# First expert's result through ScalarE and GpSimd in a two-layer recurrent kernel, with every step placed anew

## The reference, cut to what matters

```
xn = layernorm(x)
s  = softmax(mask_diagonal(q/H @ k.T)) @ v            # q, k, v are projections of xn
p  = softmax(xn @ gate); keep the two largest, divide by their sum      # gates, 8 experts
y  = sum over e of gate_e * (relu(xn @ W1_e + b1_e) @ W2_e + b2_e)      # all 8 experts are computed
x  = x + s * silu(y)
xn = layernorm(x)
s  = mamba(rmsnorm(xn)) + xn        # conv, silu, 16 states: st = st * exp(delta*A) + delta*B*u, y = sum(st * C)
f  = expert chosen by nearest centroid (top 1), layernorm + 128x512x128 relu MLP
x  = x + s * silu(alpha * f + (1 - alpha) * xn)
```

## Time and profile before

| | us |
|---|---|
| median of 3 runs (963.87 to 964.8) | 964.21 |
| profiled execution, own time | 966.05 |
| its span, first to last instruction | 964.2 |
| DVE busy | 786.6 (82%) |
| PE busy, PEld busy | 831.5 (86%), 571.5 (59%) |
| ACT busy, POOL busy | 630.8 (65%), 601.5 (62%) |
| granted TensorE clock, mean | 0.941 |

### The profile page before, as it was taken

The page is one execution under the profiler, slowest core; times in us unless marked ns, Lnnn a source line. Parts: engine busy times, 40 slices in busy tenths (PEclk is TensorE's granted clock), DMA queues, the critical chain, the costliest instruction groups (busy, mean ns, idle before and its releaser), DMA issues. The chain is left out here.

```text
span 964.2 us, 15734 instructions
## 1 busy us (share of the span) xinstructions
PE 831.5 (86%) x4576; PEld 571.5 (59%) x4576; DVE 786.6 (82%) x1503; ACT 630.8 (65%) x1379; POOL 601.5 (62%) x556
## 2 busy tenths in 40 slices
PE   5987798998799978998799969997899865876995
PEld 3773376775477745775577646864577544544552
DVE  3234637989988998899998998899889999978994
ACT  2434645878668776878577866877687854675561
POOL 0010202758857695958766795759685888778664
PEclk9987799999999999999999999999999998876997
DMA  7200103224323243324322342334331433243441
GB/s 263 95 12 1 34 12 96 78 66 121 117 66 101 90 116 109 88 77 137 102 78 78 100 125 79 88 94 114 97 100 70 124 112 97 77 108 119 138 121 45
DMA packets 79430, 90.29 MB, mean 94 GB/s; under 512 B 8450, under 2 KB 49906, under 8 KB 78834
## 3 DMA queue, kind: packets, MB, share of 16 engines
q1 hardware_dynamic: 77298, 85.07, 28.9%
q0 software_dynamic: 2048, 4.20, 1.5%
HBM read 52.96 MB, written 13.04 MB: 68 GB/s over the span
## 5 line engine op out<-in xcount | busy, mean ns | idle before, releaser
L1502 POOL TENSOR_TENSOR st<-st,Cs 128x512 f32<-128x512 f32 x249 | 316.6, 1285 | 154.7 <-DVE st L1325 152.7
L961 ACT ACTIVATE dA<-delta,Aneg 128x512 f32<-128x512 f32 x256 | 176.9, 720 | 13.6 <-POOL du L1463 9.3
L1325 DVE TENSOR_TENSOR_SCAN st<-dA,b_row 128x512 f32<-128x512 f32 x123 | 148.8, 1210 | 9.3 <-POOL y L1509 7.3
L1325 DVE TENSOR_TENSOR_SCAN st<-dA,dbu 128x512 f32<-128x512 f32 x128 | 154.7, 1209 | 2.0 <-PE yacc L905 1.9
L1509 POOL TENSOR_TENSOR y<-y,st 128x512 f32<-128x512 f32 x105 | 138.8, 1322 | 3.9
L841 PEld LDWEIGHTS work<-w_w2a,hid 128*128 128x128 f32 x1024 | 121.3, 192 | 22.7 <-DVE delta L1293 7.0
L835 PE MATMUL work<-xnT,w_w1a 128*128 128x512 f32 x256 | 134.7, 630 | 0.0
L905 PE MATMUL yacc<-st,w_ident 128*128 128x512 f32 x208 | 116.0, 647 | 14.7 <-POOL st L1502 9.6
L841 PE MATMUL work<-w_w2a,hid 128*128 128x128 f32 x1024 | 125.7, 276 | 2.6 <-DVE delta L1293 2.0
L961 ACT ACTIVATE hsT<-work,hs 128x128 f32<-128x128 f32 x352 | 99.9, 367 | 41.6 <-PE work L866 41.3
L866 PEld LDWEIGHTS work<-xsT,hs 128*128 128x128 f32 x704 | 93.1, 199 | 54.8 <-issue 37.3
(11 more groups left out here) (191 smaller groups left out, 1319.0 us busy)
## 6 DMA issues: line engine op xcount, KB each, us to landing
Cs<-c_dram SPq DMA_DIRECT2D x128, 256.0 KB, 3.6
hs<-w_w1f SPq DMA_DIRECT2D x88, 258.0 KB, 2.3
xs_in<-xs_dram SPq DMA_DIRECT2D x16, 256.0 KB, 2.9
ys_dram<-ys SPq DMA_DIRECT2D x16, 256.0 KB, 3.3
w_w1f<-in_w1f_dram SPq DMA_DIRECT2D x1, 2064.0 KB, 8.3
x_in<-in_x_dram SPq DMA_DIRECT2D x8, 256.0 KB, 4.9
w_w2f<-in_w2f_dram SPq DMA_DIRECT2D x1, 2048.0 KB, 12.4
kept_dram<-x_tok SPq DMA_DIRECT2D x8, 256.0 KB, 3.6
```

The costliest lines, as they stand in the source:

```text
L961: return nc.scalar.activation(out, in_, func, **k)
L1325: V.tensor_tensor_scan(state(s), dA[:, s % DECAYS], (dbu0, rows_bank(n, b))[h][:], 0.0, ALU.mult, ALU.add).then_inc(sig["scan"], 1)
L1502: G.tensor_tensor(state(s), state(s), Cs[:, b.of(NS, n) % C_BUFS], ALU.mult).then_inc(sig["P"], 1)
```

## The change

Expert 0 leaves DVE. Where DVE did four fused multiply-adds out of PSUM, ACT now evicts the bank with `Copy` and the gate as its scale into `gated`, a view of the first tile of `prob` (its attention weights have been read by then), and POOL adds that to `acc`.

```diff
+        gated = prob[:, 0].rearrange("p (i d) -> p i d", i=NT)
 # ACT
+                elif name == "m" and i == 0:
+                    filled(act, g, step, b)
+                    filled(act, g, ("p", NT - 1), b)
+                    act.wait_ge(sig["gates"], b.of(1, 1))
+                    for t in range(NT):
+                        last = go(gated[:, t], w[:, t * 128:(t + 1) * 128], ACT.Copy, scale=gates[:, t, 0:1])
+                    last.then_inc(fr, 1)
                 elif name == "s":
                     act.wait_ge(sig["smax"], b.of(NT, i + 1))
+                    if i == 0:
+                        since(act, sig["acc"], b.of(E + 1, -E))
 # DVE, step gate
                         filled(dve, g, ("gT", 0), b + -1)
+                        emptied(dve, g, ("m", 0), b + -1)
 # DVE, step m
-                elif name == "m":
-                    if i == 0:
+                elif name == "m" and i > 0:
+                    if i == 1:
                         dve.wait_ge(sig["gates"], b.of(1, 1))
-                        emptied(dve, g, ("b2", 0), b)
-                    else:
-                        dve.wait_ge(sig["acc"], b.of(E + 1, i))
+                    dve.wait_ge(sig["acc"], b.of(E + 1, i))
                     filled(dve, g, step, b)
 # POOL
+                elif name == "m" and i == 0:
+                    emptied(pool, g, ("b2", 0), b)
+                    emptied(pool, g, step, b)
+                    G.tensor_tensor(acc[:], acc[:], gated, ALU.add).then_inc(sig["acc"], 1)
```

Every row of `ROWS` and every entry of `OWN` has a new place, shift or both, and some have another bank. Two of the rows:

```diff
-    ("A", "m", 0, 0.31929, 6, 1, 7, 0),
-    ("A", "m", 7, 0.96705, 7, 1, 6, 0),
+    ("A", "m", 0, 0.30730, 0, 4, 0, 0),
+    ("A", "m", 7, 0.93254, 7, 1, 2, 0),
...
```

More of the change, by code:

```diff
@@ L335 @@
     ("A", 0): (
[4 rows of a table removed]
[4 rows of a table added]
     ),
     ("H", 0): (
-        -1.18779, -1.13573, -1.09164, -1.08398, -1.03594, -0.89467, -0.96660, -0.83534, -0.78966, -0.81791, -0.81272, -0.56441,
-        -0.78084, -0.73569, -0.76396, -0.85924, -0.68237, -0.67607, -0.57595, -0.60328, -0.61173, -0.84375, -0.80983, -0.51997,
-        -0.45727, -0.71044, -0.78180, -0.65968,
+        -1.10650, -1.13980, -1.09852, -0.77033, -0.97924, -0.88306, -0.94385, -0.78471, -0.76988, -0.74369, -0.71077, -0.54599,
+        -0.71041, -0.70861, -0.68303, -0.96618, -0.66433, -0.64530, -0.60176, -0.71869, -0.62037, -0.84304, -0.70132, -0.51193,
+        -0.51164, -0.46084, -1.07428, -0.69329,
     ),
     ("A", 1): (
[4 rows of a table removed]
[4 rows of a table added]
     ),
```

## The result

The changed kernel takes 984.24 us (median of 4 runs, 978.14 to 987.09), the kernel before 964.06 us beside it: a ratio of 1.0199 (1.015 to 1.0249). The forecast of 963.4 us was 21 us too low, and the time lies outside the range of 955 to 969.5.

A forecast was written before the change was run, and what follows sets the result against it. It took a steady stage as a loop of PE's leg (C `y` to `m1`) and DVE's leg (`m1` to C `y`); -2.7 at the start and +1.9 over five periods gave -0.8, so 963.4 us, 8-in-10 range 955 to 969.5.

The forecast's parts named there:

- Elsewhere: Stretches before the first stage, the last two stages and SP's DMAs: each put at 0, with small allowances.
- The period: Steady stage from `m1` to `m1`: 0.37 us longer (-0.1 to 0.9), +1.9 us over five periods.
- leg 1: PE's part of a steady stage, from C `y` to `m1`: 39.4 us, to change by -1.08.
- leg 2: DVE's part of a steady stage, from `m1` to the next C `y`: 66.4 us, to change by +1.45.
- the 0.48 at `xi0`: DVE's wait ahead of `xi0` after `m1`, to be filled: -0.48 us against `scan13`'s +1.93.
- the -1.08: PE between `a0` and `m1` loses `Ah6` (0.86 us) and `b7` (0.22 us) from its list.
- The start of the first stage: PE's 3.26 us wait ahead of `Fh0` goes; `b2` comes 3.1 us sooner, leaving -2.7 us at stage end.
- the relief: Rival, steady stages: less DVE work shortens each of five periods by 1.24 us; 955.3 us, chance 0.29.
- ACT's evictions: Four evictions on ACT in a steady stage: 1.14 us of work, 1.6 us of slack, 0 taken.
- POOL's add: One add on POOL, behind `p9` and ahead of `e4`: 1.25 us of work, 0 taken, 1.25 a stage at most.
- GpSimd's tail: Rival, stage end: C `y` waits 0.95 us for POOL in six stages; 968.5 us, chance 0.27 including ACT's queue.
- The last two stages: `a14` and `Fxs0` leave the stretch behind `scan31`, `Fh3` delays `b5`: 0, within 2 us, least known part.

The follow-up runs named there:

- e1: Changed kernel with the 64 one-column products put back on PE between A `m7` and `hT` of batch 0; 970.63 us, ratio 1.0062.
- e2: Kernel before with only the 64 products moved, behind H `z0` and ahead of A `xT` of batch 1; 974.16 us, ratio 1.0096.
- e12: Kernel before with A `h5` and `h6` moved behind `m1` on PE, `b7` and `scan13` left ahead of it; 969.79 us, ratio 1.006.
- e14: Kernel before with A `h6` moved on PE from ahead of `m1` to behind `xi0`; 967.97 us, ratio 1.0034.
- e16: e14 with two swaps on PE, `xi1` ahead of F `h6` and `sc0` ahead of A `m3`; 968.82 us, ratio 1.0057.
- e10: e1 with `b7` on PE and `scan13` on DVE both put ahead of `m1` again; 969.05 us, ratio 1.0038.
- e13: e4 with `m0` one scan earlier on DVE, between `scan10` and `scan11`; 969.98 us, ratio 1.0039.
- e3: Kernel before, all its places kept, with only the engines changed: `m0` evicted by ACT and added by POOL; 969.19 us, ratio 1.0068.
- e4: e1 with the engine edit undone, `m0` on DVE between `scan11` and `q4`; 980.83 us, ratio 1.0194.

## Why the prediction was wrong

**The step that failed** is in *Elsewhere*: "moves of a step or two in H of batch 0 are worth 0, within 1 us". I had compared the orders of the groups A, H, S, F and C, and P not at all. Among those moves stood 64 matmuls, 8.69 us of PE, which went out of an idle time into the chain of batch 1, where they took 13.65. A term put at 0 was worth 13.6 us of the 20 by e1, and 10.0 by e2, in the kernel before.

**The period.** Forecast +0.37 us, measured +1.2 in the stage shown and +1.6 on average, +8.2 over five. The split in two legs held as arithmetic: leg 1 falls to 38.2 to 38.6 where its clock is full, leg 2 takes `scan13` less the 0.48 at `xi0`, which is then without a wait. Three things were wrong.

First, "In the second leg DVE has no wait over the 0.48 us ahead of `xi0`", from which I took that leg to be DVE's own. The absence of a wait said that PE's results came in time, not by how much: by 0.04 us at `am`. PE's list holds the stage on from `m1` to the gate of layer 1 at the least (e12, e14, e16), so the -1.08 was a loan. It came without harm only as DVE had `scan13` to do meanwhile. In e10, without `scan13`, PE's new order and the pair adds hold the leg at 68.3 by themselves.

Second, the sum had no term for the durations of operations that stay where they are on their own engine. The new places let DVE's second pair add meet POOL's operations, and the two of leg 2 take 0.73 us more a stage. With it the sum for leg 2 is 1.93 - 0.48 + 0.73 = 2.2, and 2.0 was measured. This is read from the traces; no run moved a pair add alone.

Third, the clock. Before, leg 1 had a granted clock of 1.00 in each stage of the profiled execution. In e1 it varied, and with it the leg:

```profile
261.05:299.27 38.22, 38.07 (x235) 28.02 (x236) 32.03 (x59) 30.37 (x77) 26.63 (x27) 1.00 0.27 82
475.03:514.76 39.73, 39.70 (x240) 29.20 (x240) 32.44 (x60) 31.30 (x79) 26.63 (x27) 0.96 0.28 79
```

At 1.00 it is 38.2, the forecast; at 0.96, part of the leg at the 1.2 GHz level, 39.7. That is 0 to 1.5 us a stage for which the sum had no term. e13 shows the same pair, 38.18 and 39.70 us. Legs 1 below 1.00 show in variants of the old places too (0.98 in e2, 0.95 in e12 and e14). What brings them about no run settles.

**The start of the first stage.** Forecast -2.7 at its end. e1 shows it without the products: `Fh0` came 2.8 us sooner (153.2 to 150.4), as reasoned, but `b2` only 1.0 (159.3 to 158.3), `m1` 2.3 (194.8 to 192.5), and C `y` 0.1. What was late next was a bank. PE after:

```profile
166.66 1.16 PE L867 MATMUL work<-xsT,hs 128*128 128x128 f32 x8 [0.47 <-ACT xsT L962]
170.10 2.07 PE L867 MATMUL work<-xsT,hs 128*128 128x128 f32 x8 [2.29 <-DVEq L1238]
```

The gap of the earlier trace rows has gone from ahead of `Fh0` to ahead of `Fh1`, whose bank 0 is that of `m7` and stays taken to the end of DVE's `silu`. It is bank 0 in both tables: before, the late `Fh0` hid it.

**What held.** `m0` off DVE is worth 0 in the new places (e13 against e1) and less than 0 in the old ones (e3), and so the relief, the largest rival at 0.29, was rightly below the forecast; so the rule of the Trainium skill ("Perfetto Trace Analysis", section "Identifying the Most-Contended Engine"), by which the engine with the highest occupancy comes first, would have misled here: DVE was relieved of 1.2 of its 97 us a stage, and where PE didn't wait for the bank no run gained by it. Its busy time didn't even fall: 97.50 us in the stage after, 96.61 before, as the operations that meet POOL's took longer. ACT's evictions took 1.14 us. POOL's add took 1.72, over a third more than its term, and nothing waited for it in the steady stages. GpSimd's tail didn't decide. The last two stages moved by -1.2 us, within the 2 allowed; but in e1, which has the same places there, they moved by -3.5 (162.7 us), so that term was less sure than it looks.

## What to carry to other kernels

Where a whole order is laid anew, list every step that moved, the one-off ones too, and price each by its own duration and by whether its old place was idle time; 64 small matmuls in the setup outweighed everything in the steady stages. A consumer that shows no wait isn't thereby the bound: look how long its input had been ready, and if that is some hundredths of a microsecond, two engines hold the stretch together and work moved within it comes back. When an engine's relief seems to pay, look who releases which bank first. And where steps of two engines move against each other, look at the durations of those that didn't change: they are part of the price.
